# A gated residual on one core: the third chunk loaded by four DMAs, the first store moved to ScalarE's queue

## What is computed

```python
h = silu(cond @ W1.T + b1)
gate = sigmoid(h @ W2.T + b2)[:, None, :]
levels = int(log2(N))                 # N = 128
# Haar transform of x along its second axis, `levels` levels;
# the last average and every detail are multiplied by gate;
# then the inverse transform, giving a
out = x + v + a                       # v = x
```

## Time and profile before

| what | value |
|---|---|
| median of 3 runs | 166.62 us (166.6 to 166.67) |
| profiled execution, its own time | 166.82 us |
| its span, first to last instruction | 165.1 us |
| bytes moved by DMA | 69.47 MB, 421 GB/s over the span |
| DVE busy | 80.0 us, 48% of the span |
| PE busy | 22.7 us, 14% |
| ACT busy | 2.5 us, 2% |
| share of 16 DMA engines: SP's queue (q1), ACT's queue (q10) | 61.4%, 36.9% |

### The profile page before, as it was taken

One profiled execution on the slowest core, in us unless ns is written; L12 is line 12 of the kernel. 1 busy time (PEld: TensorE's weight loads), 2 busy tenths in 40 slices (PEclk: granted clock), 3 DMA queues, 4 the chain that ended last, 5 costly groups with the idle time before them and its releaser, 6 DMA issues.

```text
span 165.1 us, 219 instructions
## 1 busy us (share of the span) xinstructions
PE 22.7 (14%) x68; PEld 12.2 (7%) x68; DVE 80.0 (48%) x20; ACT 2.5 (2%) x3; POOL 2.6 (2%) x10
## 2 busy tenths in 40 slices
PE   0099969800000000000000000000000000000000
PEld 0093722300000000000000000000000000000000
DVE  0052380499999999999970000000004999700000
ACT  3000100100000000000000000000000000000000
POOL 6000000000000000000000000000000000000000
PEclk9999987995555555555555555555555555555555
DMA  5999969969998997989997996999899799799995
GB/s 151 474 456 508 476 286 508 508 286 476 508 397 365 508 508 254 508 349 413 508 429 334 508 508 302 461 508 413 349 508 445 334 492 508 318 445 405 445 421 254
DMA packets 1732, 69.47 MB, mean 421 GB/s; under 512 B 194, under 2 KB 194, under 8 KB 324
## 3 DMA queue, kind: packets, MB, share of 16 engines
q1 hardware_dynamic: 1008, 43.25, 61.4%
q10 hardware_dynamic: 724, 26.22, 36.9%
HBM read 35.92 MB, written 33.55 MB: 421 GB/s over the span
## 4 chain that ended last, share of the span: by engine, by line
DMA 50%; DVE 19%; PE 12%; DVEq 5%; ACT 1%; issue 0%
DMA ring<-in_x 23%; DMA out<-ring 22%; DVE ring L242 10%; DVE ring L247 5%; DVEq L30 5%; DMA ring<-in_L_cond_W 5%; PE gate_sum L173 3%; PE turned L181 2%; PE hidden_sum L151 2%; PE turned L135 2%; DVE ring L229 2%; PE hidden_sum L146 1%; PE turned_cond L140 1%; DVE factor L237 0%; DVE ring L222 0%; ACT ring L193 0%
## 5 line engine op out<-in xcount | busy, mean ns | idle before, releaser
L242 DVE TENSOR_TENSOR ring<-ring,factor 128x16384 f32<-128x16384 f32 x3 | 51.5, 17220 | 0.0
L247 DVE TENSOR_TENSOR ring<-ring,factor 128x8192 f32<-128x8192 f32 x2 | 17.3, 8688 | 40.5 <-DMA ring<-in_x 40.5
L216 DVE COPY ring<-turned 128x512 f32<-128x512 f32 x4 | 2.8, 692 | 10.0 <-PE turned L135 10.0
L237 DVE TENSOR_SCALAR factor<-turned 128x512 f32<-128x512 f32 x4 | 2.8, 691 | 6.9 <-PE turned L181 6.9
L173 PE MATMUL gate_sum<-ring 128*128 128x512 f32 x8 | 5.4, 833 | 1.3 <-DVE ring L227 1.3
L135 PE MATMUL turned<-identity,ring 128*128 128x128 f32 x16 | 3.6, 423 | 8.4 <-DMA ring<-in_L_cond_W 8.4
L229 DVE COPY ring<-turned 128x512 f32<-128x512 f32 x4 | 3.9, 1056 | 0.0
L135 PEld LDWEIGHTS turned<-identity,ring 128*128 128x128 f32 x16 | 3.3, 227 | 8.4 <-issue 8.4
L181 PE MATMUL turned<-ring 128*128 128x512 f32 x8 | 3.7, 601 | 0.8 <-ACT ring L193 0.8
L151 PE MATMUL hidden_sum<-ring 128*128 128x512 f32 x8 | 3.7, 605 | 0.0
L222 DVE TENSOR_TENSOR ring<-hidden_sum,ring 128x512 f32<-128x512 f32 x1 | 0.7, 692 | 5.6 <-ACT ring L190 5.6
(11 more groups left out here) (17 smaller groups left out, 6.6 us busy)
## 6 DMA issues: line engine op xcount, KB each, us to landing
out<-ring ACTq DMA_DIRECT2D x2, 4096.0 KB, 20.8
ring<-in_L_cond_W ACTq DMA_DIRECT2D x1, 1024.0 KB, 7.7
ring<-in_L_cond_W SPq DMA_DIRECT2D x1, 1024.0 KB, 7.5
ring<-in_cond SPq DMA_DIRECT2D x1, 256.0 KB, 7.7
ring<-in_x SPq DMA_DIRECT2D x3, 34.6
b_row<-in_L_cond_b ACTq DMA_DIRECT2D x2, 2.0 KB
out<-ring SPq DMA_DIRECT2D x2, 45.6
ring<-in_x ACTq DMA_DIRECT2D x1, 38.6
```

What stands on the lines that cost most here:

```text
L216: dve.tensor_copy(w1_t[:, c, :], turned[c][:, :]).then_inc(w1_t_set, 1)
L242: dve.tensor_tensor(ring[:, c, :, :], ring[:, c, :, :], steps_of(c, STEPS), ALU.mult).then_inc(chunk_scaled, 1)
L247: dve.tensor_tensor(ring[:, 0, piece(h), :], ring[:, 0, piece(h), :], steps_of(CHUNKS - 1, PIECE), ALU.mult).then_inc(chunk_scaled, 1)
```

## The change

L2 is cut into four DMAs of 8 rows each (`SMALL = 8`), issued one after the other in SP's queue, so that one run is 16 KB. All four count up the same semaphore, and DVE waits for the sum. S0 leaves SP's queue. ACT issues it instead, after the second sigmoid and a wait for the first multiply, as two DMAs: the first 8 rows of each partition (runs of 16 KB), then the other 24 rows (runs of 48 KB). Both count up `chunk_stored[0]`, and ACT waits for both before it issues L3. SP's queue issues S1 after L2, without S0 between them. The last wait for chunk 0's store goes, since ACT has already waited for it. Bytes, multiplies and all work for the gate are as before.

```diff
+SMALL = 8
@@ sync
             sp.wait_ge(gate_spread, GROUPS)
-            sp.dma_start(ring[:, SCRATCH, :, :], chunk(x_parts, SCRATCH)).then_inc(chunk_loaded[SCRATCH], DMA_DONE)
-            for c in range(SLOTS - 1):
-                sp.wait_ge(chunk_scaled, c + 1)
-                sp.dma_start(chunk(out_parts, c), ring[:, c, :, :]).then_inc(chunk_stored[c], DMA_DONE)
+            for i in range(STEPS // SMALL):
+                rows = slice(i * SMALL, (i + 1) * SMALL)
+                sp.dma_start(ring[:, SCRATCH, rows, :],
+                             chunk(x_parts, SCRATCH)[:, rows, :]).then_inc(chunk_loaded[SCRATCH], DMA_DONE)
+            sp.wait_ge(chunk_scaled, 2)
+            sp.dma_start(chunk(out_parts, 1), ring[:, 1, :, :]).then_inc(chunk_stored[1], DMA_DONE)
@@ scalar
-            act.wait_ge(chunk_stored[0], DMA_DONE)
+            act.wait_ge(chunk_scaled, 1)
+            for rows in (slice(0, SMALL), slice(SMALL, STEPS)):
+                act.dma_start(chunk(out_parts, 0)[:, rows, :], ring[:, 0, rows, :]).then_inc(chunk_stored[0], DMA_DONE)
+            act.wait_ge(chunk_stored[0], 2 * DMA_DONE)
             act.dma_start(ring[:, 0, :, :], chunk(x_parts, SLOTS)).then_inc(chunk_loaded[SLOTS], DMA_DONE)
...
-            for c in range(CHUNKS):
+            for c in range(1, CHUNKS):
                 act.wait_ge(chunk_stored[c], DMA_DONE)
@@ vector
-                dve.wait_ge(chunk_loaded[c], DMA_DONE)
+                dve.wait_ge(chunk_loaded[c], (STEPS // SMALL if c == SCRATCH else 1) * DMA_DONE)
```

## The result

The changed kernel takes 167.91 us (median of 9, 166.94 to 168.4) beside 166.62 (median of 9, 166.52 to 167.12): 0.8% more by the medians; the ratio over all runs is 1.0059, with a 95% interval of 1.0042 to 1.0076. That is above the forecast of 166.9 and outside of its range. The nine times fall in groups: 166.94 to 167.12 three times, 167.91 twice, 168.29 to 168.4 four times. The profiled execution took 168.33.

A forecast was written before the change was run, and what follows sets the result against it. The prediction took the sum of all DMA packets as the bound: 166.82 plus 0.19 (L2's cut), 0.06 (S0's cut) and 0.02 gave 167.09; the profiled execution stood 0.20 above the median, so 166.9 us, range 165.9 to 167.5.

The forecast's parts named there:

- the sum: All packets on the DMA engines set the end: 166.82 + 0.19 + 0.06 + 0.02 = 167.09 for an execution like the profiled one.
- the forecast's own range: Kernel time if the main forecast holds: 166.75 to 167.1 us, chance 0.50.
- The hand-over: Where a load is followed by the first store, packets take longer: 0.86 us an engine, expected to stay, near 54 us.
- the rival that let it go: With S0 in another queue, the stall at the first store goes: 166.0 us; chance 0.24, gone or mostly gone.
- the span given: Landing of L2, slowed by turns with S0 and L3: 86.5 to 92.5 us, given as 86 to 92 for the profile.
- The rival on the other side: Between 54 and 83 us, small load and store runs in turn cost more than alone: mostly 167.0 to 168; chance 0.13.
- The forecast's reckoning: S0, issued at 51.2 and flowing from 53.8 in turns with L2, lands at 83.0, or 83.9 with the hand-over.
- The engines standing still: L2 starved until DVE is late: engines stand still if L2 lands past some 106; at 110 about 171 us; chance 0.02.
- A start-up for each DMA: Each of four added DMAs pays 2.55 us in the stream: +10.2, 177 us; chance 0.02.
- Slower: Chance that the changed kernel is slower than before beyond the 0.33 us bound: 0.13 + 0.04 + 0.10 = 0.27.

The follow-up runs named there:

- e2: The change with S0 moved to ACT's queue as one DMA and L2 as one DMA, no small runs; 167.27 us, ratio 1.0034.
- e3: The change with L2 as one DMA; S0 stays in ACT's queue as 8 and 24 rows; 169.86 us, ratio 1.0185.
- e4: The change with S0 in one piece in ACT's queue, L2 still in four DMAs; 168.16 us, ratio 1.0069.
- e5: The kernel before the change plus one 64 KB write to the output near 9 us, waited for before L3; 166.86 us, ratio 1.0006.
- r2: The changed kernel run a third time, nothing altered; 169.57 us.
- e1: The kernel before the change with L2 in four DMAs of 8 rows, S0 whole in SP's queue; 166.75 us, ratio 1.0008.
- e8: The kernel before the change with S1 as two DMAs of 16 rows and L3 waiting for the first of them; 166.88 us, ratio 1.0008.
- e7: The kernel before the change with S1 cut into two DMAs of 16 rows; 166.94 us, ratio 1.0012.
- run 64: Not a run or kernel: the words are from "15 engines already run 64 KB packets of S1", where "run" is a verb; no time.
- r1: The changed kernel run once more for a second trace, nothing altered; 167.17 us.
- e9: The kernel before the change with S1 held until S0 has landed, so S1 and L3 start together; 179.34 us, ratio 1.076.
- e10: The kernel before the change with S1 held until S0 has landed and two small loads are done; 170.74 us, ratio 1.0247.
- e6: The change with S1's issue held until S0 has landed; 178.5 us, ratio 1.071.

## Why the prediction was wrong

**Right.** The kernel is bound by what its DMA engines carry, and it stayed so. 16 KB cost 0.615 and 48 KB 1.816 where 0.611 and 1.815 were forecast from other sizes, and where nothing else happened the sum came out: the low group of times, 166.94 to 167.17, lies beside the forecast's 166.9, two of its four times in the forecast's own range and the others within 0.07 of it. The engines take from two queues packet by packet, shown by e2, e3 and e4, in which L2 lands at 79.7, 70.5 and 97.1 by run size alone. The hand-over stayed (0.76 an engine), as the forecast took it and the rival that let it go did not; only the reason given for it, being the first store, is refuted by e5. L2 landed at 85.5, just before the span given.

**The step that failed.** "So the end is the sum of all packets on the DMA engines, provided that some queue always has work." The proviso held, and the sum held for 14 or 15 engines of 16. But the last store is done when the slowest engine is done, and its packets are not all of one price. In the profiled execution one engine ended 1.3 us after the rest, in e2's one 1.0 us, in r2 two, 2.1 and 2.3 us. The sum put this at nothing: it has no term for engines that come apart. This is the missing term: by difference 1.0 of the 1.3 us between the medians, the rest being the packets' 0.27.

**Where it comes from.** e1 has L2's small runs without the move and 166.75; e2 has the move without small runs and 167.27, spread as after. e8 rules out that L3 is late, and so does r2, in which it wasn't late. What is left is that S0 flows beside L2, in turns, for some 20 to 30 us. The rival on the other side named this stage ("small runs of load and store in turn are dearer than alone") and came near in size, but not in kind: small runs weren't needed, and for most engines the stage is not slower (0.615 and 1.816 a packet). The excess falls on one or two engines. A part comes in the stage itself (0.9 us in e2 at 57.2, 0.4 and 0.9 us in r2), the rest after it, mostly on packets of L3.

That moving the store makes an engine late, and that the late engine makes the time, is shown. That it is the mixing rests on elimination (gone in e1, e7 and e8) and on those slow packets within it. One rival was not tried by itself: the move also changes how far S1 is ahead when L3 joins, at 64 KB a run. Against it stands r2: its two late engines had S1 two and three packets ahead, as the engines of before, and each had had slow packets by then. How the mixing leaves one engine open to disturbance 5 to 60 us later is not shown. In all three traces of the changed kernel the late engine was also the last to finish S0, one turn behind the others, and so it was in e2. The DMA view of the changed kernel shows it, from 86 to 88.9 us: 15 engines already run 64 KB packets of S1 and one still has its 48 KB packet of S0.

```profile
q1 hardware_dynamic: 15, 0.98, 78.2%
q10 hardware_dynamic: 1, 0.05, 3.9%
```

That the slip leads to the slow packets was not tried.

**S0 landed at 91.9, not 83.9.** 3 us of it are that S0 was issued at 54.3, since PE's matmuls of the first layer took 6.56 us in this execution (line 154 in the chain; 3.65 before), which delayed the gate. 5 us are turns: the semaphore's packet takes a turn of its own. From 88.95 to 89.6 us 15 of them run, one 64 KB packet of S1 after S0's last data; the sixteenth follows at 91.3 or later, because its engine was a turn behind.

```profile
DMA packets 31, 1.05 MB, mean 1613 GB/s; under 512 B 15, under 2 KB 15, under 8 KB 15
...
q10 hardware_dynamic: 15, 0.00, 1.3%
```

The forecast's reckoning had left both out. In r1 and r2, with S0 issued at 52.5 and 52.4, it landed at 87.5 and 88.3. Nothing hung on it, since L3 at 127.4 was still in time for S3.

**The other rivals.** The engines standing still did not happen in the change; e3 shows it happening at 104 to 107 us by another way than I had priced (S0 starved, not L2), for 1.8 us. The case against that rival was also weaker than it reads: it ends at 102, one us past its own bound of 101. A start-up for each DMA: e1 has three DMAs more and is 0.12 above its own before, so it is not paid in a filled queue. The Trainium skill (SBUF — State Buffer, "The DMA setup-cost knee") has a fixed 2 us for each transfer; taken as a price in a stream, e1's 0.12 disagrees. The Trainium skill's round robin by packet (DMA: Bandwidth & Descriptors, "Queues, rings and completion order") is what the landings of e2 to e4 show.

**Chances.** Slower had 0.27 and the range ended at 167.5. With 13% for dear mixing I had read "no cost" out of a single stretch, S1 beside L3, which e9 shows to be luck in how far S1 was ahead, and not the rule.

## What to carry to other kernels

When a kernel is bound by its DMA engines, add up each engine's packets and then ask what can set one engine back, for the last one decides; count the semaphore packets of the last DMA over short stretches to see it. Don't let a store flow beside a load merely because it can: where one queue already kept the engines full, a second gave no bandwidth here, only risk. And where a load and a store must run together, try their offset: starting both at the same moment cost 7 to 8% here, the pause before them included, and with the store two packets ahead (before) or the load five (e10) the packets kept their price.

## What was not expected of the hardware

- Turning from a stretch of loads alone to stores cost each DMA engine 0.4 to 1.4 us: 0.86 in before, 0.76 after, 0.7 in e5, 0.5 in e2 (16 packets of L2 from 53.9 to 54.8 us), 0.4 and 1.2 in e3, 1.4 in e10. With stores beside the loads until just before the turn it cost nothing (L3 to S2 in before). Nor did it in e2, where L3 ran alone for five or six packets before S2: from 112 to 134 us 144 data packets took 99.2% of 22 us on 16 engines, 2.42 each. So a stretch of loads alone isn't enough; what else it takes is open.

```profile
q10 hardware_dynamic: 160, 9.44, 99.2%
```

- L3 and S1 running packet by packet one apart over their chunks (e6, e9) slow each other to 2.80 us a packet of 64 KB; with the load five ahead, or the store two ahead, it is 2.42. Why one place is bad (the memory behind it, or the moment) is open: only these offsets were tried.
- A semaphore's packet waits for its turn like data: beside 64 KB packets in the other queue it costs a landing up to 2.4 us.
